# A 1024-step coherent scan: vectors carried by VectorE and ScalarE, or scalars with dot products from a Gram matrix

## What is computed

```python
xs = (msk_n.transpose(2, 0, 1), best.transpose(1, 0, 2), maxc.T)
def step(prev, inp):
    mn, bst, mx = inp
    prev_n = prev / (jnp.linalg.norm(prev, axis=-1, keepdims=True) + EPS)
    d_ad = jnp.maximum(jnp.sum(mn * prev_n, axis=-1), 0.0)
    cur = (d_ad[:, None] * prev + mx[:, None] * bst) / (d_ad + mx + EPS)[:, None]
    return (cur, cur)
_, gen = jax.lax.scan(step, jnp.zeros((b, c), x.dtype), xs)
```

## Time and profile before

| | us |
|---|---|
| median of 3 runs | 15209.85 |
| lowest, highest | 15209.34, 15213.14 |
| span of the profiled execution | 15214.5 |
| PE, DVE, ACT, POOL busy in it | 9980.4, 9300.2, 7945.1, 5137.7 |
| first dot product of the scan starts | 12636.54 |
| last reciprocal of the scan starts | 14869.82 |
| granted TensorE clock, mean | 0.836 |

### The profile page before, as it was taken

The page is one execution under the profiler, slowest core; times in us unless marked ns, Lnnn a source line. Parts: engine busy times, 40 slices in busy tenths (PEclk is TensorE's granted clock), DMA queues, the critical chain, the costliest instruction groups (busy, mean ns, idle before and its releaser), DMA issues. The chain is left out here.

```text
span 15214.5 us, 295101 instructions
## 1 busy us (share of the span) xinstructions
PE 9980.4 (66%) x105986; PEld 7080.0 (47%) x105986; DVE 9300.2 (61%) x20130; ACT 7945.1 (52%) x14451; POOL 5137.7 (34%) x3844
## 2 busy tenths in 40 slices
PE   8655657999999998778777799866846770000002
PEld 3253223777777776666666688623223330000002
DVE  3213435777777777888888533225444547888882
ACT  5211223777777776566666422352334436777770
POOL 0003334556555555333333355300007891000001
PEclk9878878999999999999999999997878885555555
DMA  6787674111111111011111399978996661000008
GB/s 252 197 171 216 213 233 156 42 42 42 40 41 41 42 42 58 28 67 45 67 45 67 138 364 363 328 264 310 376 386 226 206 205 42 12 12 12 12 12 310
DMA packets 1245925, 2176.95 MB, mean 143 GB/s; under 512 B 99573, under 2 KB 900997, under 8 KB 1177605
## 3 DMA queue, kind: packets, MB, share of 16 engines
q1 hardware_dynamic: 813156, 1637.88, 32.9%
q10 hardware_dynamic: 410912, 463.54, 8.6%
q0 software_dynamic: 20608, 58.22, 1.5%
HBM read 1369.30 MB, written 790.14 MB: 142 GB/s over the span
## 5 line engine op out<-in xcount | busy, mean ns | idle before, releaser
L781 POOL TENSOR_TENSOR la_s<-la_s,la_mx 128x512 f32<-128x512 f32 x2048 | 2093.0, 1043 | 1462.7 <-DVE la_mx L740 1462.3
L2147 PE MATMUL fp_tp<-fp_idn,fp_f 128*128 128x128 f32 x512 | 89.6, 348 | 2547.0 <-DMA fp_f<-ft 2529.7
L820 ACT ACTIVATE la_et<-la_pt 128x512 f32<-128x512 f32 x2048 | 1119.0, 598 | 732.2 <-PE la_pt L652 732.1
L652 PE MATMUL la_pt<-la_idn,la_s 128*128 128x128 f32 x8192 | 1164.5, 287 | 220.5 <-POOL la_s L781 219.8
L2147 PEld LDWEIGHTS fp_tp<-fp_idn,fp_f 128*128 128x128 f32 x512 | 79.9, 184 | 2557.3 <-issue 2340.8
L740 DVE TENSOR_REDUCE la_mx<-la_s 128x16 f32<-128x1024 f32 x1024 | 1243.2, 1214 | 17.7
L732 DVE TENSOR_TENSOR la_s<-la_ps,la_post 128x2048 f32<-128x2048 f32 x512 | 1167.9, 2281 | 27.9 <-PE la_ps L638 27.7
L652 PEld LDWEIGHTS la_pt<-la_idn,la_s 128*128 128x128 f32 x8192 | 913.5, 145 | 334.2 <-issue 231.8
L1439 PE MATMUL pj_pp<-pj_pw,pj_at 128*128 128x256 f32 x4096 | 926.4, 379 | 0.0
L2133 POOL DMA_INDIRECT ft<-fp_g,fp_idx x64 | 62.2, 971 | 2503.4 <-DMA fp_g<-gen 2486.3
L956 PE MATMUL gm_xp<-gm_fws,gm_y 128*128 128x258 f32 x2048 | 559.7, 420 | 421.8 <-ACT gm_ri L1040 421.8
(11 more groups left out here) (298 smaller groups left out, 28104.7 us busy)
## 6 DMA issues: line engine op xcount, KB each, us to landing
f_xt<-in_x SPq DMA_DIRECT2D x128, 1024.0 KB, 8.0
i_xr<-in_x SPq DMA_DIRECT2D x64, 2048.0 KB, 9.1
x<-pj_o SPq DMA_DIRECT2D x64, 2048.0 KB, 10.2
f_xt<-x SPq DMA_DIRECT2D x128, 1024.0 KB, 14.1
i_xr<-x SPq DMA_DIRECT2D x64, 2048.0 KB, 14.6
x<-i_xo ACTq DMA_DIRECT2D x64, 2048.0 KB, 14.5
sp_xt<-x SPq DMA_DIRECT2D x144, 512.0 KB, 4.6
out<-sp_xt SPq DMA_DIRECT2D x144, 512.0 KB, 2.9
```

The source lines that it names most:

```text
L652: last = nc.tensor.transpose(t_bank(S, i)[:, h, :], s[:, S % RS, i, h, :], idn[:, :])
L781: nc.gpsimd.tensor_tensor(sv, sv, mb, ALU.subtract).then_inc(s_sub, 1)
L820: nc.scalar.activation(et[:, k % RT].rearrange("p h n -> p (h n)"), t_bank(S, i)[:, :, :].rearrange("p h n -> p (h n)"), ACT.Exp).then_inc ...
```

## The change

The scan is rewritten. A row is held as a numerator that is a weighted sum of the scaled best rows; its dot product with any later row is the same weighted sum of dot products between stored rows. These come from `gram`: for tiles of 128 rows, PE makes the products of each scaled best row with the normalised rows and the scaled best rows of its own tile and the first 16 of the next (`gram_products`), ACT halves them into `gs`, SP stores them and loads, per step, 2x32 of them into `g` (16 loads per tile, `load_gram`). DVE carries `w`, 2x33 numbers per image: the dot products of the current numerator with the coming rows. A step multiplies `w` by the step's weight and adds the step's line of `g`, one shift to the left being done by the offset of the buffer. ACT has one root in a step. The weight of every step stands in `tt`.

Every 16 steps (a batch) a few more things happen. PE spreads the 16 weights over 128 partitions (`broadcast`, 16 small products), DVE makes the 16 numerators of all images with one prefix scan over 128 x 272 numbers in the layout feature by step (`spread_scan`, after step 3 of the next batch), ACT copies the last numerator into a block-diagonal (`carry`), PE makes from it the dot products with the rows of the batch after (`entering`, 32 small products of 8x16), and DVE adds them to `w` (`switch`). ACT copies the numerators to `gt` (`collect`), PE turns them back to rows and ACT scales them by 1/den (`rows`), which SP stores. In the batches 1 to 4 of the 8 in a tile, two images' Gram products of the next tile are made.

`select_points` now stores `mnt` and `mbt`, features on partitions. `mnt` is the first part of `tc`, which exists already; for `mbt` PE makes 16 transposes per image (`turn_best`) and ACT four copies of 128x512 with a factor 2 (`double_best`); the stores of `mn` and `mb` are gone.

```diff
@@ select_points, ScalarE and TensorE @@
                     last.then_inc(s_mbs, 1)
-                    act.wait_ge(s_mbs, b + 1)
-                    act.dma_start(mb[b].rearrange("(t p) h -> p t h", p=P), best[:, :, :]).then_inc(s_mb, 16)
...
+                    for n in range(4):
+                        r, t0 = n // 2, n % 2 * 4
+                        act.wait_ge(s_bp, 4 * b + n + 1)
+                        nc.scalar.activation(bt[:, r, t0 * P:(t0 + 4) * P], bp[n % 2][:, :], ACT.Copy, scale=2.0).then_inc(s_bt, 1)
+                    act.wait_ge(s_bt, 4 * b + 4)
+                    act.dma_start(mbt[b].rearrange("r p n -> p r n"), bt[:, :, :]).then_inc(s_mb, 16)
...
@@ coherent_scan, SyncE @@
+                def load(T):
+                    for q, src in enumerate((mnt, mbt)):
+                        sp.dma_start(vt[:, T % 3, q, :, :], src[:, :, :, T * P:(T + 1) * P].rearrange("b r p n -> p (b r) n"))\
+                            .then_inc(s_vt[T % 3], 16)
...
+                        for q in range(2):
+                            sp.dma_start(g[:, T % 2, i * K:(i + 1) * K, q, 1:1 + c],
+                                         gram[T, :, i * K:(i + 1) * K, q, i * K:i * K + c]).then_inc(s_g[T % 2], 16)
...
@@ coherent_scan, TensorE @@
+                def broadcast(n):
+
+                    pe.wait_ge(s_t, (n + 1) * K)
...
+                def entering(n):
+
+                    if n + 2 < NB:
+                        pe.wait_ge(s_d0, n + 1)
...
+                for n in range(NB):
+                    T, i = n // KT, n % KT
+                    for place in gram_places(n):
+                        gram_products(*place)
+                    if T:
+                        if i == 0:
+                            lengths(T - 1)
+                        rows(T - 1, i)
+                    broadcast(n)
+                    entering(n)
...
@@ coherent_scan, ScalarE @@
+                    act.wait_ge(s_h, s + 1)
+                    nc.scalar.activation(sm[:, (s + 1) % 2, 7:8], sm[:, s % 2, 0:1], ACT.Sqrt, bias=gq[:, T % 2, s % P:s % P + 1],
+                                         scale=tt[:, s:s + 1]).then_inc(s_root, 1)
+                    if k == 5 and n:
+                        carry(n - 1)
+                    if k == 6 and n:
+                        collect(n - 1)
+                    if k == 7 and n + 1 < NB:
+                        addends(n + 1)
+                    if k in (9, 11):
+                        for place in gram_places(n)[(k - 9) // 2:(k - 9) // 2 + 1]:
+                            gram_evict(*place)
...
+                    if k == 13 and T:
+                        rows(T - 1, i)
...
@@ coherent_scan, VectorE @@
-                            nc.vector.scalar_tensor_tensor(num[:, o, :], y[:, i, :], inverse, mbt[:, j, k, :],
-                                                           ALU.mult, ALU.add).then_inc(s_num, 1)
...
+                    nc.vector.scalar_tensor_tensor(t, inv[i], 0.0, p_[i], ALU.max, ALU.mult).then_inc(s_t, 1)
+                    dve.wait_ge(s_t, s + 1)
+                    nc.vector.scalar_tensor_tensor(h[i], sq[i], t, w[:, now, 1, 1 + k:2 + k], ALU.mult, ALU.add).then_inc(s_h, 1)
+                    nc.vector.scalar_tensor_tensor(den, dd[:, s:s + 1], t, mxe[:, s:s + 1], ALU.mult, ALU.add).then_inc(s_den, 1)
+                    nc.vector.scalar_tensor_tensor(w[:, then, :, 0:c], w[:, now, :, 0:c], t, g[:, T % 2, s % P, :, 0:c],
+                                                   ALU.mult, ALU.add).then_inc(s_w, 1)
+                    dve.wait_ge(s_h, s + 1)
+                    nc.vector.scalar_tensor_tensor(sq[o], h[i], t, gq[:, T % 2, s % P:s % P + 1], ALU.mult, ALU.add).then_inc(s_sq, 1)
+                    dve.wait_ge(s_den, s + 1)
+                    nc.vector.reciprocal(r, den).then_inc(s_r, 1)
+                    if s + 1 < NMASK:
+                        if k == K - 1:
+                            switch(n, then, (s + n + 2) % 3)
+                        dve.wait_ge(s_r, s + 1)
+                        nc.vector.scalar_tensor_tensor(rho[o], r, -1.0, r, ALU.mult, ALU.max).then_inc(s_rho, 1)
...
+                        dve.wait_ge(s_w, s + 1)
+                        nc.vector.tensor_scalar(wp[o], wn, r, 0.0, ALU.mult, ALU.max).then_inc(s_wp, 1)
+                        dve.wait_ge(s_rho, s + 1)
+                        dve.wait_ge(s_root, s + 1)
+                        nc.vector.tensor_scalar(length[o], root[o], rho[o], CSA_EPS, ALU.mult, ALU.add).then_inc(s_len, 1)
+                        dve.wait_ge(s_wp, s + 1)
+                        nc.vector.tensor_tensor(p_[o], wp[o], r, ALU.mult).then_inc(s_p, 1)
+                        dve.wait_ge(s_len, s + 1)
+                        nc.vector.reciprocal(inv[o], length[o]).then_inc(s_inv, 1)
+                    if k == 3 and n:
+                        spread_scan(n - 1)
```

More of the change, by code:

```diff
@@ new lines, in rows @@
+                def rows(T, b):
+                    n = T * B + b
+                    act.wait_ge(s_tp, n + 1)
+                    if b == 0:
+                        act.wait_ge(s_rt, T + 1)
+                    if n >= 2:
+                        act.wait_ge(s_store[b % 2], 16 * (n // 2))
+                    nc.scalar.activation(go[:, b % 2, :], tp[n % 2][:, 0:H], ACT.Copy, scale=rt[:, T % 2, b:b + 1]).then_inc(s_go, 1)
+                for b in range(B):
+                    gram_evict(0, b)
@@ L2035, in _ @@
+                collect(NB - 1)
+                lengths(NT - 1)
+                for b in range(B):
+                    rows(NT - 1, b)
             @block.vector
             def _(dve):
[L2037 to L2042 removed]
@@ new lines, in _, with squares @@
+                dve.wait_ge(s_init, 8)
+                h, sq, rho, wp, p_, length, inv, root = ([sm[:, i, c:c + 1] for i in range(2)] for c in range(8))
+                nc.vector.memset(w[:, 0, 0, 0:1], 1.0).then_inc(s_init, 1)
+                nc.vector.memset(inv[0], 0.0).then_inc(s_inv, 1)
+                dve.wait_ge(s_init, 9)
+                dve.wait_ge(s_inv, 1)
+                def squares(T):
+                    dve.wait_ge(s_g[T % 2], 16 * 2 * KT * (T // 2 + 1))
+                    gv = g[:, T % 2, 0, 1, 1:2]
+                    diagonal = bass.AP(gv.tensor, gv.offset, [gv.ap[0], [K * 2 * (WIN2 + 1), KT], [2 * (WIN2 + 1) + 1, K]])
+                    nc.vector.tensor_scalar(gq[:, T % 2, :].rearrange("p (i k) -> p i k", i=KT), diagonal, 0.5, 1e-30,
+                                            ALU.mult, ALU.add).then_inc(s_gq, 1)
+                    dve.wait_ge(s_gq, T + 1)
```

373 lines of the change are left out of this document (262 added, 111 removed).

## The result

The changed kernel takes 14689.67 us (median of 4 runs, 14687.5 to 14692.61) against 15211.49 for the kernel before beside it (4 runs, 15209.34 to 15218.77). In the profiled executions the span fell from 15214.5 to 14685.3 us, by 529.2.

The account below looks back on a forecast made before the run. The scan's 2233.3 us, closed off by barriers, was taken as exposed, its step bound by a dependent chain. Scan -418, start +36, end +18, `select_points` +4 sum to -360: 14854.5, as median 14850 us; range 14700 to 15030.

Parts of the forecast that it names:

- the ring: Chain of dependent instructions in one scan step: through DVE and ACT before, all on DVE after, forecast at 1.70 us a step.
- (a): On DVE, an instruction without a wait starts 0.07 us before the recorded end of the one ahead.
- (b): On DVE, an instruction that waits for its predecessor's semaphore starts 0.04 us after that predecessor's end.
- the first rival: Scan step on DVE: any wait stops the overlap, so each instruction costs its full duration; 2.5 us a step, about 15670; 5%.
- Rule (c): On DVE, an instruction that waits for two semaphores starts 0.07 us later still.
- a cheaper step: Rival for the scan step: waits already there cost nothing and L2354 not 0.07; 1.60 us, -102, 14750; 10%.
- Durations (d): DVE instructions on single numbers: 0.15 us with tensor operands or a reciprocal, 0.20 with one pointer scalar, 0.26 with two.
- Switch: DVE's extra rows behind `r` every 16 steps: 0.4 us, 63 times, 25 us.
- Prefix scan: DVE's scan of 272 numbers every 16 steps: 0.46 us, 63 times, 29 us; upper bound 58 us.
- Pauses and lateness: Scan extras: 13 us for pauses of 0.25 us, 5 us for ACT batches waiting on PE (bounds 0 and 20).
- The rival of late batch work: PE's small products take 0.3 us, so ACT and the root stand in 28 batches: +110, 14960; 13%.
- Start: Before the first scan step: `vt` loads 20, Gram products 16, `g` loads 8, together 44 us; +36, bounds +22 and +60.

## Why the prediction was wrong in size

The direction, the mechanism and the place were right: the 256-wide rows leave, the ring lies on DVE alone, and nothing of the batch work holds it. By its steps:

- **Rules (a) and (b)** hold in the changed step. `sq`, `r`, `wp` and `p` wait for semaphores that are long there and start 0.07 us before the recorded end of the row ahead. That refutes the first rival, that each instruction is paid in full (2.5 us a step). The Trainium skill, page "VectorE: DVE Perf Modes", section The DRAIN you can't avoid, has the next operation wait until the pipe is empty, and adds that one which is not held starts earlier. The trace agrees with the addition: the overlap is 0.07 us here, as it was in the earlier trace rows.
- **Rule (c) is the step that failed.** It was read from one row, L2063, whose wait row is for the reciprocal just ahead and so the last to come. It was then put on `length`, whose wait row, for the root, comes early. In the changed kernel the root ends at 0.81 us and `length` starts at 1.16, and the wait row is taken ahead of time. This is the 0.08 us of `length`, and the extra waits of `switch` and prefix scan fell with it. A second row of the old step, L2070, paid 0.09 us for a wait row whose semaphore was up; so the rule was not baseless, but in the changed step no register operation stands there, and the wait row is taken beside the rows ahead of it. The prediction held this case as its rival "a cheaper step", 1.60 us with 10%, and then put only part of it into the range.
- **Durations (d)** were rounded up: 193 ns were taken as 0.20, 136 as 0.15, and a start 0.035 us after the end taken as 0.04. Each is under 15 ns; over eleven rows they are the other 0.05 of the 0.133 us. Together the step was mis-sized by 1024 x 0.133 = 136 us, of the 155 by which the scan was better than forecast.
- **Switch:** 0.205 us instead of 0.4, 12 us less. Its two extra waits, 0.14 us by rule (c), cost nothing, and the memset is taken beside the row that was to wait behind it. **Prefix scan:** 0.63 instead of 0.46, 11 us more, well inside the bounds 0.46 and 0.92. The row that the prediction cited from the Trainium skill (page "DVE: opcode table, instruction layouts, handler registers and perf-mode slots", section Datapath and trigger behaviour: half throughput) agrees with the 0.72 us measured; by it the term would have been 18 us more, and 11 more came, since the three extra waits that the term also held (0.21 us, 13 in all) cost nothing.
- **Pauses and lateness:** 18 us forecast, 4 with the squares measured. The 13 us for pauses do not follow from their own figures, which give 18 (a tenth of 1024 steps, 0.25 us, scaled by 13200/19000). The rows that were to show lateness of the root show none: L2354 has 1.3 us of idle time in front of it in the whole scan.

```profile
L2354 DVE TENSOR_SCALAR cs_sm<-cs_sm 8x1 f32<-8x1 f32 x1023 | 196.1, 192 | 1.3 <-issue 1.2
```

- **The rival of late batch work** was wrong at `entering` (1.88 us, where it had 9.6 and the forecast 2.6 to 6.7) and right in kind at the Gram products, 3.4 us an image where 1.7 was taken. They still don't hold ACT.
- **Start:** +50.7 instead of +36, inside the bounds of +22 and +60. The products are the term: 27.5 us where 16 were forecast. The earlier trace rows were misread there. The transposes are one row each, so 0.21 was taken as the price of a product; a product of f32 numbers has two rows, as the pair on the second line of the earlier trace rows already showed. The same mistake made `broadcast` 3.4 instead of 7.0 us at the end.
- **`select_points`:** -10.5 instead of +4. Of this, 3 us are seen in the last image: the transposes and copies do cost there, but `mx`, whose landing was the last thing before (13.3 us behind its issue), now starts ahead of them. The prediction listed the two stores as gone or replaced and didn't ask when the third one starts. The other 7 us lie earlier. The three profiled executions with the old code in this stage have 1162.9 to 1168.1 us there, the six with the changed code 1155.7 to 1158.1, so the two groups do not overlap, and part of the gain is the change's. The old code with only `mx` stored first has 1159.3, so most of the gain may be that one store; one profiled execution does not show it. The stages ahead have the same code in all kernels: in the ten profiled executions they take 11436.4 to 11460.9 us, and the kernel before is the slowest.

The parts add up: -155 in the scan, -25 in the stages ahead, +15 at the start, -4 at the end, with rounding the -169 by which the span was better than forecast. The first term is the error; with the step as measured (136 us less) and without the five extra waits of `switch` and prefix scan (22 us) the forecast would have been about 14690.

## What to carry to other kernels

On a ring of tiny DVE instructions, count distances of starts and not durations: a dependent row starts 0.035 us after the end of what it needs, an independent one 0.07 before the end of the row ahead, so put a row that nobody waits for behind each row that is waited for (124 us here), but only as long as the other engine's answer still comes in time. Where a row waits for two semaphores, write the wait that ends last first, since it stays on the row itself, while the second wait is a row of its own that costs 0.07 us if it comes last. Have register operations worked out ahead of both waits and well ahead of the row: one between the waits took the first of them and cost 0.09 us. Price small matrix products by the columns of their weights and by two passes for f32, and issue a scattered store before anything that can hide it (4 us in the trace here, too little to show in the time).
